# A decoder layer on one core: zeros multiplied at the start, keys stacked from a second queue, and five pieces of work at other places

## What is computed

```python
x = x + attn(layernorm(x), w_atten, w_proj)       # q, k, v = split(x @ w_atten.T); rope(q), rope(k)
                                                  # softmax(q k^T / sqrt(32), causal) v @ w_proj.T
query = context @ Wq.T + bq;  key = context @ Wk.T + bk
x = x + softmax(query @ key.T, axis=-1) @ layernorm(x)
h = layernorm(x)
shared = (silu(h @ Ws_gate) * (h @ Ws_up)) @ Ws_down
routed = sum over the two best experts e of  p_e * (silu(h @ We_gate[e]) * (h @ We_up[e])) @ We_down[e]
x = x + routed + shared
```

## Time and profile before

| | |
|---|---|
| median of 3 runs | 1061.14 us (1059.96 to 1066.61) |
| profiled execution | 1060.61 us |
| its span, first to last instruction | 1058.8 us |
| mean granted TensorE clock | 0.989 |
| TensorE busy | 1001.7 us, 95% |
| VectorE, ScalarE, GpSimd busy | 600.7, 483.2, 182.3 us |

### The profile page before, as it was taken

The page is one execution under the profiler, slowest core; times in us unless marked ns, Lnnn a source line. Parts: engine busy times, 40 slices in busy tenths (PEclk is TensorE's granted clock), DMA queues, the critical chain, the costliest instruction groups (busy, mean ns, idle before and its releaser), DMA issues.

```text
span 1058.8 us, 17800 instructions
## 1 busy us (share of the span) xinstructions
PE 1001.7 (95%) x6016; PEld 749.2 (71%) x6016; DVE 600.7 (57%) x1603; ACT 483.2 (46%) x1267; POOL 182.3 (17%) x209
## 2 busy tenths in 40 slices
PE   6998999999999999998789999989999999999998
PEld 4456555655556565564567698878988889889997
DVE  5597567774688646775535368334324442444565
ACT  1477664755647556565541241234424442442221
POOL 3222101220112111120000011011111111112342
PEclk9999999999999999999889999999999999999999
DMA  8777254442643525425500031542444425413554
GB/s 222 116 144 115 41 73 61 60 62 81 119 61 44 77 80 80 53 35 126 171 21 20 21 110 41 206 163 74 160 162 161 143 78 162 162 66 124 162 190 157
DMA packets 69130, 111.23 MB, mean 105 GB/s; under 512 B 6144, under 2 KB 30720, under 8 KB 69056
## 3 DMA queue, kind: packets, MB, share of 16 engines
q1 hardware_dynamic: 63456, 91.92, 37.1%
q0 software_dynamic: 5600, 18.35, 5.9%
HBM read 59.66 MB, written 25.43 MB: 80 GB/s over the span
## 4 chain that ended last, share of the span: by engine, by line
PE 74%; DVE 11%; DMA 7%; issue 4%; ACT 2%; POOL 1%; DVEq 0%; SPq 0%; ACTq 0%; POOLq 0%
PE ps L1204 21%; PE ps L1214 11%; PE ps L976 9%; PE ps L1023 6%; DMA ks<-rope_a 5%; PE ps L1120 5%; PE ps L1062 4%; PE ps L996 3%; PE ps L1046 3%; PE ps L1010 3%; DVE gu_lo L1512 2%; DMA routed_x<-xn_d,table_cur 2%; PE ps L924 2%; PE ps L1082 2%; PE ps L1222 2%
## 5 line engine op out<-in xcount | busy, mean ns | idle before, releaser
L761 ACT COPY probsT<-ps 128x128 f32<-128x128 f32 (+3 forms) x256 | 108.5, 424 | 143.4 <-PE ps L1023 140.9
L1363 DVE CUSTOM_DVE_ANT_0 probs<-ps,mask 128x128 f32<-128x128 f32 (+3 forms) x256 | 123.5, 487 | 87.7 <-PE ps L1010 63.7
L1010 PE MATMUL ps<-ks,qs 96*128 96x256 f32 (+2 forms) x256 | 143.5, 565 | 12.8 <-DMA ks<-rope_a 9.5
L753 ACT ACTIVATE probs<-probs,nb 128x128 f32<-128x128 f32 (+3 forms) x256 | 145.9, 570 | 20.8 <-DVE nb L1368 20.1
L976 PE MATMUL ps<-xnT,wqk 128*128 128x512 f32 (+1 forms) x272 | 125.7, 579 | 1.7 <-ACT xnT L741 1.4
L1023 PE MATMUL ps<-ident,probs 128*128 128x128 f32 x640 | 115.9, 280 | 0.2
L855 ACT ACTIVATE sg<-ps 128x352 f32<-128x352 f32 x69 | 32.0, 464 | 171.1 <-PE ps L1204 171.0
L1023 PEld LDWEIGHTS ps<-ident,probs 128*128 128x128 f32 x640 | 77.9, 142 | 35.2 <-issue 29.3
L1644 DVE TENSOR_TENSOR hidden<-sg,ps 128x352 f32<-128x352 f32 x69 | 35.8, 518 | 116.6 <-ACT sg L855 116.6
L651 POOL TENSOR_TENSOR rope_a<-rope_a,sin_sb 128x512 f32<-128x512 f32 (+1 forms) x34 | 41.1, 1209 | 282.2 <-DVE rope_a L1345 282.2
L1010 PEld LDWEIGHTS ps<-ks,qs 96*128 96x128 f32 x256 | 49.0, 192 | 55.8 <-issue 27.4
(11 more groups left out here) (161 smaller groups left out, 1930.7 us busy)
## 6 DMA issues: line engine op xcount, KB each, us to landing
gu_raw<-in_we SPq DMA_DIRECT2D x10, 1408.0 KB, 6.8
y_d<-y_sb SPq DMA_DIRECT2D x37, 256.0 KB, 2.4
shared_x<-xT_d SPq DMA_DIRECT2D x32, 256.0 KB, 2.8
qs<-rope_b SPq DMA_DIRECT2D x30, 256.0 KB, 5.0
ks<-rope_b SPq DMA_DIRECT2D x30, 256.0 KB, 6.8
d_raw<-in_we SPq DMA_DIRECT2D x10, 512.0 KB, 7.7
xn_d<-xn SPq DMA_DIRECT2D x4, 1024.0 KB, 4.3
xT_d<-xn_xT SPq DMA_DIRECT2D x16, 256.0 KB, 3.2
```

Source lines behind the costliest of these rows:

```text
L753: nc.scalar.activation(pr, pr, ACT.Exp, bias=nb[:, n % 2, h:h + 1], scale=SCALE, accum_out=sums[:, n % 2, h:h + 1]).then_inc(exp_done, 1)
L761: nc.scalar.copy(probsT[n % 2][:, h, 0:w], ps[:, T_BANK + h % 2, 0:w]).then_inc(pT_done, 1)
L1010: nc.tensor.matmul(ps[:, S_BANK + h % 2, 0:w], stacks[G % 2][0][:, h, i * P:(i + 1) * P], stacks[G % 2][1][:, h, 0:w], start=True, stop=Tr ...
L1363: nc.vector.tensor_tensor_reduce(probs[n % TT][:, h, 0:w], ps[:, S_BANK + h % 2, 0:w], mask[:, TOKENS - w:], 1.0, LOWEST, ALU.add, ALU.max ...
```

## The change

It does these things:

- TensorE waits for the mask's memset, now the first of GpSimd's, and multiplies 128x128 of its zeros 13 times into the score bank before it waits for the constants.
- The copies of group 0's keys into the stack are issued by ScalarE (`stack_first_keys`), after its four `copy_first_turned` and before everything else; SP keeps the queries'.
- The query's sum of most groups moves from place 8 to 4 (`ROPE_SUM`), that of a batch's first group from 51 to 49 (`FIRST_ROPE_SUM`).
- Group 15, the last, gets tables of its own: keys at 2, 2, 4, 4 instead of 3, 5, 7, 7, their products at 4 instead of 7, sums at 3 and 6 instead of 8 and 9. (The tables `EARLY_...` are now called `OWN_...`.)
- In `CROSS` the context keys move from place 7 to 9, their copy from 9 to 10, the first two energies and maxima from 10, 11 to 11, 12, the first exponential from 11 to 12, the first division from 13 to 14. `LAST_CROSS` keeps its places but for the last two of these.
- `normalise` stands behind `mask_and_max` and ahead of the rope, norm and cross work of its place.
- ScalarE does a Silu of one column, into a tile that nothing reads, between the attention and the shared expert.

```diff
-ROPE_RAW, ROPE_SUM = (1, 7), (8, 9)
+ROPE_RAW, ROPE_SUM = (1, 7), (4, 9)
-FIRST_ROPE_RAW, FIRST_ROPE_SUM = (47, 53), (51, 55)
+FIRST_ROPE_RAW, FIRST_ROPE_SUM = (47, 53), (49, 55)
...
+OWN_QUERIES = {1: (1, 1, 1, 4), 2: (-2, -2, -1, 0), 3: (-11, -9, -6, -2), 4: (46, 47, 47, 48),
+               15: (-1, -1, 1, 1)}
+OWN_KEYS = {1: (3, 7, 7, 7), 2: (0, 2, 3, 3), 3: (-1, 1, 3, 3), 4: (48, 49, 51, 51), 15: (2, 2, 4, 4)}
+OWN_RAW = {1: (5, 8), 2: (0, 5), 3: (0, 7), 4: (49, 55), 15: (1, 4)}
+OWN_SUM = {1: (7, 10), 2: (3, 8), 3: (3, 9), 4: (51, 57), 15: (3, 6)}
...
 CROSS = dict(
-    context=(2, 7), context_copy=(7, 9),
-    energy=(10, 11, 14, 15), energy_max=(10, 11, 14, 15), energy_exp=(11, 14, 15, 21), energy_divide=(13, 18, 21, 25),
+    context=(2, 9), context_copy=(7, 10),
+    energy=(11, 12, 14, 15), energy_max=(11, 12, 14, 15), energy_exp=(12, 14, 15, 21), energy_divide=(14, 18, 21, 25),
 LAST_CROSS = dict(
-    CROSS, energy_exp=(11, 14, 15, 16), energy_divide=(13, 18, 19, 20),
+    CROSS, context=(2, 7), context_copy=(7, 9), energy=(10, 11, 14, 15), energy_max=(10, 11, 14, 15),
+    energy_exp=(12, 14, 15, 16), energy_divide=(14, 18, 19, 20),
...
             for half, done in enumerate((stacked_first, stacked)):
-                for i in range(2):
-                    stack_high(0, i, half, HALVES[half], done)
-                    stack_low(0, i, half, HALVES[half], done)
+                stack_high(0, 0, half, HALVES[half], done)
+                stack_low(0, 0, half, HALVES[half], done)
...
+            def stack_first_keys(half, done):
+                cols = HALVES[half]
+                act.wait_ge(rope_high, unit(0, 1, half) + 1)
+                for j in (0, 2):
+                    act.dma_start(stacks[0][1][j * HDIM:(j + 1) * HDIM, :, cols].bitcast(F32), rope_b[1][:, cols])\
+                        .then_inc(done, 16)
+                act.wait_ge(rope_done, unit(0, 1, half) + 1)
+                act.dma_start(stacks[0][1][HDIM:2 * HDIM, :, cols].bitcast(F32), rope_a[1][:, cols]).then_inc(done, 16)
             for t in range(TT):
                 copy_first_turned(0, t)
+            for half, done in enumerate((stacked_first, stacked)):
+                stack_first_keys(half, done)
             for place in range(FFN_PLACE):
                 attend(place)
             turn(shared, 0)
+            nc.scalar.activation(silu_unused[:], bias_sb[:, 0:1], ACT.Silu)
...
+            pe.wait_ge(zeroed, 1)
+            for _ in range(WARM):
+                nc.tensor.matmul(ps[:, S_BANK, 0:P], mask[:, 0:P], mask[:, 0:P], start=True, stop=True)
             pe.wait_ge(consts, 3)
...
                     mask_and_max(r, h)
+                n = step_at(place, WEIGH_LAG)
+                if h == GH - 1 and n is not None and n % TT == TT - 1:
+                    normalise(n // TT)
...
```

31 lines of the change are left out of this document (13 added, 18 removed).

## The result

| | before | changed |
|---|---|---|
| median | 1061.78 us (4 runs, 1059.96 to 1066.61) | 1053.12 us (4 runs, 1051.95 to 1054.51) |
| ratio | | 0.992, 95% interval 0.9894 to 0.9946 |
| profiled span | 1058.8 us | 1050.1 us |
| mean granted clock | 0.989 | 0.992 |

The change makes the kernel 8.7 us faster. The forecast was 1041, with a range of 1034 to 1050: the direction was right, but 19.7 us of gain were forecast and less than half of that came. The rest of this document is about the missing 11 us.

A forecast was written before the change was run, and what follows sets the result against it. TensorE, busy 1001.7 of 1058.8 us, was taken as the bound, leaving its waits and the clock to gain. Terms 3.4 + 3.5 + 1.7 + 4.2 + 1.6 + 3.6 + 0.7 + 2.0 - 1.0 = 19.7 gave 1041 us, range 1034 to 1050.

The forecast's parts named there:

- The opening: Kernel start: zero products raise the clock (2.6 us), key copies on ScalarE's queue issue sooner (1.0); 3.4 us taken.
- Query sums and last keys: Group starts: earlier sums and last-group products land keys sooner, 4.9 us less 1.4 in costs, 3.5 us gain.
- the clock's 1.7: Last group: granted clock of 0.83 around the 3.70 us wait counted as regained, 1.7 us.
- I put 0.6 + 0.8 = 1.4 us on that: Last group: cost of keys waiting for the query's raw copy and rope products ahead of the second norm's scaling.
- The small losses: VectorE: moved query sums ahead of the second norm's scale in three batches, ScalarE's extra loads included, -1.0 us.
- The O bank: Weighing with values: earlier normalise removes five bank waits, 4.2 us, and shortens the one at 513.7 us by 1.6.
- The context keys: Batch starts: keys at place 9 remove two waits for the router's shift r_t, 3.6 us gain.
- Copy and energies move with it: Context keys: assumed their copy and energies follow the keys' move two places later, leaving 3.6 us gain.
- The SiLU: Shared expert: first silu starts earlier with the context Exp behind it, shrinking the 2.83 us wait for hidden by 0.7.
- The clock at 510 to 550: After attention: 6.9 us lost to lowered clock, of which 2.0 us would come back.
- (b): Rival: moved sums on VectorE delay the masks that TensorE's scores wait for; 14 us lost, 1054 us, chance 0.11.
- (c): Rival: moved sums on VectorE also stall and drop the clock in every group; slower, 1072 us, chance 0.02.

The follow-up runs named there:

- e16: e11 plus eight products of ident with itself ahead of group 3's first scores, where TensorE waits for the keys: 1037.10 us, ratio 0.9761.
- experiments 13 to 15: The kernel before, the changed kernel and e11, each profiled a second time unchanged; e11 again took 1038.87 us, ratio 0.977.
- experiment 7: The kernel before with only the query sums moved, to places 4 and 49: 1057.05 us, ratio 0.9952.
- experiment 2: The changed kernel with context keys, their copy and the energies back at the places of the kernel before: 1050.04 us, ratio 0.9875.
- e11: Changed kernel, last group on common tables, place-8 sums moved early only for groups 10, 14, 15 (last: place 3), both context copies at 10, first value product at 9: 1037.97 us.
- e5: The changed kernel with the first context copy at place 10 and the last group on the common tables: 1044.74 us, ratio 0.9847.
- experiment 9: Unused SiLU removed from the changed kernel with last group on common tables, context keys at 8, copies and first value product at 9: 1041.55 us, against 1041.97 with it.
- e13: The kernel before, unchanged, profiled a second time; the text gives its half-speed stretches but no time of its own.
- e6: The kernel before with only normalise moved ahead of the rope products and sums: 1054.65 us, ratio 0.9943.
- e4: The changed kernel without the 13 products of zeros, ScalarE's key queue kept: 1056.55 us, ratio 0.9931.
- e12: The changed kernel with the first group's key copies back on SP's queue, zeros kept: 1051.82 us, ratio 0.9918.
- e3: The changed kernel with the last group's own tables removed, so it uses the common ones with the query sum at place 4: 1048.33 us, ratio 0.9871.

## Why the prediction was wrong

**The opening: the sum right, the split in part luck.** 3.4 forecast; 4.32 at the first scores in the profile above, 3.2 to 4.3 over eleven of the twelve profiles with both edits (2.2 in e16), and 3.3 at place 16 in the mean of nine. The zeros give 3.1 (forecast 2.6) and the queue at most 0.5 (forecast 1.0): the issue did come 1.0 us sooner, and the landing, taken as unchanged, took 0.8 us more. Unforeseen: the landing waits at group 1 and 3 grew by 0.42 and 0.5 us (0.79 to 1.21, 2.15 to 2.65), because their transfers don't start as much sooner as TensorE arrives.

**Query sums and last keys: the gain right, the price wrong.** The landing waits gave 1.17 + 1.24 at groups 10 and 14 and the whole 3.70 at group 15, more than the 4.9 forecast; the clock's 1.7 came too (5.53 between places 236 and 252), and here it did belong to the wait, as experiments 13 to 15 show. The step that failed is "I put 0.6 + 0.8 = 1.4 us on that": the last group's tables cost 4.0 us beyond the sum. It named both waits rightly and took both too small: the one for the raw copy, which reads the query out of the QK bank, was 1.30 us and not 0.6, and the one for the second norm's scaling 1.62 and not 0.8; about 1 us more went in steps that no wait shows. And the query sum at place 4 was nearly enough alone, which the earlier trace rows would have said: 3 us sooner against a wait of 3.70.

**The small losses: term mis-sized.** Forecast -1.0 in three batches; the sums cost 4.2 us (experiment 7). The term had three batches, one place in each, and ScalarE's loads; the sums cost at four places (68, 100, 164 and 228), and 0.9 to 1.25 us each. VectorE "57% busy over the span", as the prediction has it, is an average: at these places what stands behind the sum is wanted by TensorE within a place or two. At the other seven places of moved sums it cost nothing.

**The O bank: right.** 4.2 + 1.6 forecast; 4.85 + 1.43 measured alone, 4.84 + 1.98 in the changed kernel's first profile, where a half-speed stretch at 507.0 us stands ahead of the last wait and covers 0.55 of it; the second profile has 1.44.

**The context keys: the main error.** The step that failed is "Copy and energies move with it", on which the 3.6 stood. Forecast +3.6, measured -5.8 (experiment 2), a swing of 9.4 us out of 11 missing. Three things were not followed: (1) "Copy and energies move with it" is wrong in the table: the energies do, the first copy does not, and its wait is for both products. The question that the step lacked is what else waits for the moved instruction, and what is queued behind that waiter (4.5 us). (2) The 1.98 us product at place 7 was itself the cover for the QK bank that the values of place 8 need; moved away, that wait comes out (1.02 us, three times, worth 1.3 us each by the scores of e11 against e5). (3) In batch 1 there was no r_t wait to win, and all the costs were paid. With 4.5 and 3.9 us lost and 3.9 of r_t won, 1.3 us of the 5.8 stay without a named cause.

**The SiLU: 0.7 forecast, 0.68 measured**, with the right reason as far as experiment 9 can tell by exclusion (the exponential behind the first silu). That the two added loads are covered held too: the kernel without them is no faster. Their price is the 1.28 us of the row and no more: in the changed kernel the load starts at 518.42 us, as soon as the cast ahead of it ends, and the SiLU at 519.72.

**The clock at 510 to 550: mostly one draw.** Behind place 252 the changed kernel's profile gains 5.5 us besides the waits for yT and hidden, against 2.0 forecast. Of it 1.6 stand at a wait for a transfer of the routed experts (L1192 before, 4.5 us; L1211 after, 2.9), which the change does not touch and which is 2.5 to 4.5 us long over all profiles; the rest goes with three half-speed stretches fewer. But the two profiles of the kernel before have 23.9 and 20.5 us at half speed, those of the changed one 17.1 and 6.8. The earlier trace rows was read as a property of the kernel. Counted by 3.4 us, the four profiles without the whole change (before, e13, e6, e7) have 5 to 7 stretches, 5.8 in the mean, and the fourteen others 2 to 7, 4.1 in the mean. So there are somewhat fewer with fewer long waits; no more than that can be booked, and how many an execution has stays open.

**The ledger.** Forecast: 19.7. The context keys took 9.4, the last group's tables 2.6 (4.0 for 1.4), the sums 3.2, the early landings 0.9, and the stretch at 90.6 us 1.7: -17.8. Landing waits gave 1.3 more (7.9 for 6.6 with the clock), the opening 0.9, the O bank 1.0, and the stretches and the transfer behind place 252 3.5: +6.7. 19.7 - 17.8 + 6.7 = 8.6, against 8.7 between the two spans. Of the rivals, (b) named VectorE's sums ahead of the scores and was partly at work (4.2 of its 14 us); none named ScalarE, which carried the largest single loss. In (c) the sum is off by one: 3.1 us for each of ten sums ends at 1071 (31 less the 20.7 of gain), not 1072.

## What to carry to other kernels

When an instruction is moved later, list everything that waits for its semaphore, read the *count* that each of them waits for, and ask what is queued behind that waiter on its in-order engine: a copy that waited for both of two products turned a move on TensorE into a 4.77 us stall on ScalarE. Ask as well what the moved work was covering where it stood; a 2 us product is also a 2 us pause in which a bank comes free. And move work only for the instances whose wait the trace shows: sums moved for three groups gave all the gain, at three other groups they cost 2.8 us. Last, before a slow stretch of the clock is booked to a kernel, take a second profile of the same kernel.

## What the runs showed of the hardware

- Products of zeros raise TensorE's clock: it was granted in full from between 4.3 and 7.4 us on with 13 of them from 1.35 us on, from between 13.1 and 14.5 us on without.
- The same program has another number of half-speed stretches from one execution to the next, some at the same places and some not. A wait of 1.6 to 2.7 us can be followed by one, and the same wait can go without (2.65 us: seven of twelve profiles). A stretch of 3.4 us cost 1.7 us where TensorE was the limit and 0.33 us where VectorE was (469.5 us of the changed kernel). Two profiles of the changed kernel differed by 2.6 us in span (1050.1 and 1047.5), with the same long waits in both.
- A SiLU put ahead to load its table did nothing where an Exp stood between it and the first real one: three loads of 1.28 us instead of one, and the same 2.15 us wait with and without it.
- The last 128 KB copy of the keys, issued 1.0 us sooner from a second engine's queue, took 5.17 us to land instead of 4.35 (e4 and before), and 4.5 instead of 3.2 in the median of two (changed and e12).
- With the queries' copies 3 us ahead of them the keys' last copy took 10.1 us to land, with four more places between them 6.8 us (before and e3).
